# A decoder layer on one core: keys spread over four places, queries kept twice, x copied to PSUM by ScalarE, the maxima split in PSUM

## What is computed

```python
# 1. state-space mixer, 256 inner channels, 16 states each
x_h, res = split(layernorm(h) @ W_in.T);  x_h = silu(conv4(x_h))
dt, B, C = split(x_h @ W_x.T);            dt = softplus(dt @ W_dt.T + b_dt)
h_t = exp(dt_t * A) * h_{t-1} + dt_t * B_t * x_t          # scan over time
y_t = sum_states(h_t * C_t) + D * x_t
x = x + (inner residual) + alpha * (y * silu(res)) @ W_out.T
# 2. cross attention, 16 heads of 8 channels, 64 keys, masked
x = x + softmax(mask(q k^T / sqrt(8))) v @ w_o.T + b_o
# 3. eight experts, the two best of each token, 128 -> 512 -> 128 with relu
x = x + sum_top2(p_e * (relu(h W1_e + b1_e) W2_e + b2_e))
```

## Time and profile before

| | |
|---|---|
| median of 3 runs | 883.64 us (881.62 to 884.72) |
| the profiled execution | 876.18 us, its span 874.4 us |
| TensorE, matmuls | 693.3 us busy, 79% |
| VectorE | 714.5 us, 82% |
| ScalarE | 523.7 us, 60% |
| GpSimd | 629.3 us, 72% |
| mixer rounds | about 30 to 627 us |
| experts' groups, with the last attention | about 637 to 874 us |

### The profile page before, as it was taken

The page is one execution under the profiler, slowest core; times in us unless marked ns, Lnnn a source line. Parts: engine busy times, 40 slices in busy tenths (PEclk is TensorE's granted clock), DMA queues, the critical chain, the costliest instruction groups (busy, mean ns, idle before and its releaser), DMA issues. The chain is left out here.

```text
span 874.4 us, 12132 instructions
## 1 busy us (share of the span) xinstructions
PE 693.3 (79%) x3795; PEld 468.9 (54%) x3795; DVE 714.5 (82%) x1059; ACT 523.7 (60%) x1251; POOL 629.3 (72%) x467
## 2 busy tenths in 40 slices
PE   6567569778888787988878796776779889789991
PEld 4343335445555355545545553553457568689991
DVE  3679999999999999999999999999943644645684
ACT  3777549667966975887796697666125234223330
POOL 1358889688889898988988999898812334464554
PEclk9778869999999999999999999987899999899996
DMA  4535595463537447434632653654073325648773
GB/s 101 194 111 156 171 290 152 156 185 133 186 108 229 154 156 214 157 112 150 193 133 107 211 160 104 198 172 147 26 224 107 122 95 158 215 166 307 220 245 101
DMA packets 80410, 142.69 MB, mean 163 GB/s; under 512 B 10555, under 2 KB 53574, under 8 KB 80346
## 3 DMA queue, kind: packets, MB, share of 16 engines
q1 hardware_dynamic: 75802, 133.38, 48.1%
q0 software_dynamic: 4544, 8.54, 2.8%
HBM read 110.25 MB, written 37.27 MB: 169 GB/s over the span
## 5 line engine op out<-in xcount | busy, mean ns | idle before, releaser
L1451 POOL TENSOR_TENSOR prod<-hst,BC 128x1024 f32<-128x1024 f32 x128 | 301.5, 2362 | 65.0 <-DVE hst L1664 54.2
L1664 DVE TENSOR_TENSOR_SCAN hst<-dA,Rp 128x1024 f32<-128x1024 f32 x128 | 292.0, 2282 | 6.4
L1188 ACT ACTIVATE dA<-dtm,Aneg 128x255 f32<-128x255 f32 x512 | 214.2, 495 | 75.8 <-DVE hst L1664 74.9
L1571 POOL DMA_INDIRECT y2d<-prod,back x78 | 81.6, 1046 | 117.2 <-DVE prod L2016 101.3
L1456 POOL TENSOR_TENSOR prod<-prod 128x512 f32<-128x512 f32 x128 | 163.6, 1289 | 2.4
L1655 DVE TENSOR_TENSOR Rp<-BC,Rp 128x1024 f32<-128x1024 f32 x128 | 156.9, 1226 | 7.7 <-DMA BC<-bcd 0.6
L638 PE MATMUL Y<-prod,ident 128*128 128x256 f32 x512 | 139.1, 405 | 21.9 <-POOL prod L1456 17.0
L638 PEld LDWEIGHTS Y<-prod,ident 128*128 128x128 f32 x512 | 99.7, 202 | 57.1 <-POOL prod L1456 22.1
L638 PE MATMUL Mb<-hpad,winT 128*128 128x512 f32 (+1 forms) x176 | 83.2, 622 | 15.2 <-ACT xh L1137 11.9
L638 PEld LDWEIGHTS Rp<-BC,xh 128*128 128x128 f32 x624 | 76.0, 193 | 4.5 <-issue 2.6
L638 PE MATMUL Rp<-BC,xh 128*128 128x128 f32 x624 | 76.6, 276 | 0.6 <-DVE prod L2016 0.6
(11 more groups left out here) (266 smaller groups left out, 1170.4 us busy)
## 6 DMA issues: line engine op xcount, KB each, us to landing
BC<-bcd SPq DMA_DIRECT2D x63, 1024.0 KB, 5.6
BC<-recs SPq DMA_DIRECT2D x39, 578.0 KB, 4.2
xsd<-blank SPq DMA_DIRECT2D x17, 1056.0 KB, 12.0
dtm<-xsd SPq DMA_DIRECT2D x39, 132.0 KB, 3.8
recs<-in_L_ffn_W SPq DMA_DIRECT2D x16, 256.0 KB
xin<-in_x SPq DMA_DIRECT2D x8, 256.0 KB, 5.8
x2d<-x2o SPq DMA_DIRECT2D x8, 256.0 KB, 5.8
E<-x2d SPq DMA_DIRECT2D x4, 512.0 KB, 5.3
```

The costliest lines, as they stand in the source:

```text
L1188: m = A(dA[:, k % RING, i, 1:SEQ], dtm[:, r % 2, d, b * SEQ + 1:(b + 1) * SEQ], ACT.Exp, scale=Aneg[:, d, c * NC + i:c * NC + i + 1])
L1451: TT(prod[:, k % RING, :, :], hst[:, k % RING, :, :], BC[:, (k // 2) % BCR, 1, :, :], ALU.mult).then_inc(s_pd, 1)
L1571: pool.indirect_dma_start(out=y2d[:, :], out_offset=bass.IndirectOffsetOnAxis(ap=at, axis=0), in_=yr[:, j % YR, i, :], in_offset=None, bou ...
L1664: v.tensor_tensor_scan(hst[:, k % RING].rearrange("p n s -> p (n s)"), dA[:, k % RING].rearrange("p n s -> p (n s)"), U.rearrange("p n s - ...
```

## The change

- Kbd has 4 blocks in place of 16. Block j is KT times the sum of the four masks of heads j, 4 + j, 8 + j and 12 + j (`blk4`), so one block carries a head in each quarter of the channels. The queries are kept twice, qT[:, 0] and qT[:, 1], each with the channels of every second quarter zeroed (by `qscale` and `qbias`, per partition); the product of a 64-row half with copy w and the four blocks gives four heads. `scores` has four matmuls of 256 columns a tile instead of two of 512; `scores_t` takes the weights from the four blocks. The order of the heads in a bank changes (TRIO, `exps`).
- All `key_blocks` (four activations) stand at k = 6, in the drain at k = 7; `queries` issues two activations.
- `copy_xh` on ScalarE copies xh into DTX: for the second sequence in slot k = 6, ahead of `key_blocks`, once `inputs` of step 7 has read the old contents (s_u); for the next round's first one at k = 15, behind `decays`. `steps_x` waits for it (s_xc) and multiplies DTX by dtm in place.
- `steps_x`, `least` and `normed` move from VectorE's `middle` to its `slot`, behind the scan; `least` from k = 8 to k = 7.
- `split_max` writes the negated maxima as f32 into PSUM first (in the last round SBUF) and splits from there: five operations, where it was four.
- Five small constants are made at step 0 of round 0, and one (bq) goes.

```diff
-        TRIO = ((0, 1), (4, 5)), ((2, 3), (6, 7))
+        TRIO = ((0, 2), (4, 6)), ((1, 3), (5, 7))
...
-                    mm(T[h][:, :], qT[rows, b, t * P:(t + 1) * P], Kbd[rows, b, 8 * h:8 * h + 8, :], stop=False)
+                for w in range(2):
+                    for h in range(2):
...
+                        rows = slice(64 * h, 64 * h + 64)
+                        mm(T[h][:, w * SEQ:(w + 1) * SEQ], qT[rows, w, b, t * P:(t + 1) * P], Kbd[rows, b, :, :],
+                           start=w == 0, stop=False, skip_group_check=True)
...
-                A(qT[:, :, :].rearrange("p b s -> p (b s)"), T[1][:, :], ACT.Identity, bias=bq[:, 0:1], scale=float(HD) ** -0.5).then_inc(Ta.sem, 1)
+                for w in range(2):
+                    m = A(qT[:, w, :, :].rearrange("p b s -> p (b s)"), T[1][:, :], ACT.Identity, bias=qbias[:, w:w + 1], scale=qscale[:, w:w + 1])
+                m.then_inc(Ta.sem, 1)
...
+            def copy_xh(r, b):
+
+                if r or b:
+                    act.wait_ge(s_u, r * STEPS + b * (STEPS // 2))
+                    act.wait_ge(Aa.sem, Aa.at("xh1", r))
+                else:
+                    act.wait_ge(Ha.sem, Ha.at("xh1", 0))
+                A(DTX, xh[:, r % 2, :, b * SEQ:(b + 1) * SEQ], ACT.Copy).then_inc(s_xc, 1)
...
-                for h in range(half * HP, (half + 1) * HP):
-                    m = A(Kbd[:, :, h, :], KT[:, :, :], ACT.Copy, scale=blk[:, h:h + 1])
+                for j in range(HP // 2):
+                    m = A(Kbd[:, :, j, :], KT[:, :, :], ACT.Copy, scale=blk4[:, j:j + 1])
...
+                if k == 6 and r < ROUNDS:
+                    copy_xh(r, 1)
                 if prev and k == 6:
-                    key_blocks(r - 1, 0)
+                    key_blocks(r - 1)
...
+                if k == 15 and r + 1 < ROUNDS:
+                    copy_xh(r + 1, 0)
                 slot(r, k)
...
-                if r or b:
-                    v.wait_ge(s_u, r * STEPS + b * (STEPS // 2))
+                v.wait_ge(s_xc, r * NB + b + 1)
                 half = slice(b * SEQ, (b + 1) * SEQ)
-                v.tensor_tensor(DTX[:, :, :], dtm[:, r % 2, :, half], xh[:, r % 2, :, half], ALU.mult).then_inc(s_dx, 1)
+                v.tensor_tensor(DTX[:, :, :], dtm[:, r % 2, :, half], DTX[:, :, :], ALU.mult).then_inc(s_dx, 1)
...
-                v.tensor_scalar(nm[:, :, 0, 0:HEADS], mx[:, :, :], -1.0, None, ALU.mult).then_inc(Tv.sem, 1)
+                v.tensor_scalar(part, mx[:, :, :], -1.0, None, ALU.mult).then_inc(Tv.sem, 1)
                 v.wait_ge(Tv.sem, Tv.at("ma", r))
-                v.scalar_tensor_tensor(part, mx[:, :, :], -1.0, nm[:, :, 0, 0:HEADS], ALU.mult, ALU.subtract).then_inc(Tv.sem, 1)
+                v.tensor_copy(nm[:, :, 0, 0:HEADS], part).then_inc(Tv.sem, 1)
                 v.wait_ge(Tv.sem, Tv.at("mb", r))
+                v.tensor_tensor(part, part, nm[:, :, 0, 0:HEADS], ALU.subtract).then_inc(Tv.sem, 1)
...
+                if k == 7:
+                    steps_x(r, 1)
+                    if tail:
+                        least(r - 2)
+                if nxt and k == 15:
+                    steps_x(r + 1, 0)
+                if ln and k == 15:
+                    normed(r + 2)
```

More of the change, by code:

```diff
@@ L102, in decoder @@
         blk = sb("blk", [P, HEADS])
+        blk4 = sb("blk4", [P, HP // 2])
+        quads = sb("quads", [P, HP // 2])
         iota = sb("iota", [P, EXPERTS])
@@ L181, in decoder @@
         KT = sb("KT", [P, NB, KEYS])
-        Kbd = sb("Kbd", [P, NB, HEADS, KEYS])
+        Kbd = sb("Kbd", [P, NB, HP // 2, KEYS])
         Vg = sb("Vg", [P, NB, HP, GW])
         ones = sb("ones", [P, 2, GW])
-        qT = sb("qT", [P, NB, SEQ])
+        qT = sb("qT", [P, 2, NB, SEQ])
+        qscale = sb("qscale", [P, 2])
+        qbias = sb("qbias", [P, 2])
         sqt = sb("sqt", [P, TOK])
@@ L317, in decoder @@
         Ta = Marks(sem("Ta"), "KT V sq ln rs q m e00 e01 e10 e11 ld rd x2")
-        Tv = Marks(sem("Tv"), "xq " + " ".join(f"mx{i}a mx{i}b" for i in range(NB * QT)) + " ma mb mc me n")
+        Tv = Marks(sem("Tv"), "xq " + " ".join(f"mx{i}a mx{i}b" for i in range(NB * QT)) + " ma mb mc md me n")
         s_kb = sem("s_kb")
@@ L767, in scores @@
                 if i == 0:
-                    pe.wait_ge(s_kb, 2 * (r + 1))
-                for h in range(2):
[L770 to L774, removed]
-                    mm(T[h][:, :], qT[rows, b, t * P:(t + 1) * P], Kbd[rows, b, 8 * h:8 * h + 8, :], stop=False)
-                for h in range(2):
-                    mm(T[h][:, :], identb[:, :], mbias[:, t, :].unsqueeze(1).to_broadcast([P, 8, KEYS]), start=False).then_inc(Tp.sem, 1)
+                    pe.wait_ge(s_kb, r + 1)
+                for w in range(2):
+                    for h in range(2):
+                        if w == 0 and i:
+                            pe.wait_ge(Tv.sem, Tv.at(f"mx{i - 1}{'ab'[h]}", r))
+                        elif w == 0 and h == 0:
+                            pe.wait_ge(Ta.sem, Ta.at("q", r))
+                        rows = slice(64 * h, 64 * h + 64)
+                        mm(T[h][:, w * SEQ:(w + 1) * SEQ], qT[rows, w, b, t * P:(t + 1) * P], Kbd[rows, b, :, :],
+                           start=w == 0, stop=False, skip_group_check=True)
+                for h in range(2):
+                    mm(T[h][:, :], identb[:, :], mbias[:, t, :].unsqueeze(1).to_broadcast([P, 8, KEYS]), start=False, skip_group_check=True).then_inc(Tp.sem, 1)
             def turn_max(r):
@@ L789, in scores_t @@
                     for h in range(2):
-                        hp, rows = TRIO[g][h][i], slice(64 * h, 64 * h + 64)
-                        mm(T[h][:, i * SEQ:(i + 1) * SEQ], Kbd[rows, b, 2 * hp:2 * hp + 2, :], qT[rows, b, :],
+                        rows = slice(64 * h, 64 * h + 64)
+                        mm(T[h][:, i * SEQ:(i + 1) * SEQ], Kbd[rows, b, 2 * g:2 * g + 2, :], qT[rows, i, b, :],
                            start=i == 0, stop=False, skip_group_check=True)
@@ L1392, in _ @@
             first_half()
+            copy_xh(0, 0)
             act.wait_ge(s_pre, NPRE)
@@ L1773, in middle @@
                         logits(r - 2)
-                    if k == 8:
-                        least(r - 2)
                 if k == 11 and r < ROUNDS:
@@ L1781, in middle @@
                     maxima(r - 1, 2)
-                if k == 7 and r < ROUNDS:
-                    steps_x(r, 1)
-                if nxt and k == 15:
-                    steps_x(r + 1, 0)
-                if ln and k == 15:
-                    normed(r + 2)
             def slot(r, k):
@@ L1863, in _ @@
                 nxt_(v.tensor_copy(mbias2[:, t, :, :], mbias[:, t, :].unsqueeze(1).to_broadcast([P, 2, KEYS])))
-            nxt_(v.tensor_scalar(bq[:, :], bq[:, :], float(HD) ** -0.5, None, ALU.mult))
             assert n == NPRE
```

26 lines of the change are left out of this document (17 added, 9 removed).

## The result

The changed kernel takes **860.16 us** (median of 4 runs, 855.9 to 866.7), the kernel before 884.18 beside it (881.62 to 884.93): a ratio of 0.9746, 95% interval 0.9713 to 0.9778. Forecast were 859.6 us, 854 to 871. The profiled execution took 859.85 us, its span is 858.0.

A forecast was written before the change was run, and what follows sets the result against it. VectorE was taken to bound the round (72.77 of 75.10 us), GpSimd next. 17.5 + 1.6 + 5.9 - 1.8 + 0.8 = 24.0 us off the profile's 876.18 gives 852.2, plus 7.5 to the median: 859.6 us, range 854 to 871.

The forecast's parts named there:

- The stretch, 17.5 us: VectorE's dt*x: with x in PSUM, GpSimd can't hold it; 15 products fall from 27.7 to 10.2 us.
- The place, 1.6 us: `steps_x` behind the scan at k = 7 and 15: hides latency, 1.6 us gained beyond the stretch.
- the stretch isn't the operands: Rival at L1637 and L1688: they stretch because of where they stand, new ones alike; 883 us, chance 0.04.
- The split, 5.9 us: Maxima split on VectorE, rounds 1 to 7: five ops take 9.0 us where the old chain took 14.9.
- `least`, -1.8 us: VectorE at k = 7: `least` waits 0.3 us for GpSimd's `nl` in each of six rounds, losing 1.8 us.
- ScalarE's queue, slack 0 to 0.3 us: ScalarE at decays(10) behind `copy_xh`: fits narrowly; rival that it makes the kernel slower, 890 us, chance 0.06.
- The sign that I had named for going wrong: dA or the root named as a release before scans or `att_normed` at k = 9, 10.
- GpSimd's wait for the expert choice: GpSimd in the mixer round: its wait for VectorE's choice falls from 2.3 us to under 1.
- The drain, 0.8 us: Round 7's attention in the expert stage: fewer Kbd copies gain 1.0 us, the split's fifth op takes back 0.2.
- TensorE, 0: Scores as four 64x256 matmuls in place of two 64x512: same columns, costed at 0.
- The start, 0: Five constants at k = 0 of round 0, 1 us of work: taken as 0, at most 1.
- The sum: Whole kernel: the terms gain 24.0 us; 859.6 us forecast, chance 0.60.

The follow-up runs named there:

- e1: The changed kernel with the product dt*x reading x from SBUF again, copies, waits and place behind the scan kept: 860.87 us, ratio 0.9734.
- run 5: The changed kernel with dt*x back ahead of the scan, still in PSUM behind ScalarE's copy: 877.53 us, ratio 0.9997 to the kernel before.
- e12: The changed kernel with dt*x ahead of the scan, x from SBUF, no copies; new keys, queries and split stay: 876.44 us, ratio 0.9982.
- e3: The kernel before with only four Kbd copies, two query copies and matching score matmuls; old product and split: 879.72 us, ratio 0.9958.
- e6: The changed kernel with two more unread copies of 256 columns on ScalarE behind `copy_xh(r, 1)`: 862.96 us, ratio 0.982.
- e4: The kernel before with only `steps_x`, `least` and `normed` moved behind the scan, x from SBUF, no copy: 870.90 us, ratio 0.9841.
- e11: The changed kernel without `copy_xh` and its wait, dt*x behind the scan with x from SBUF: 852.02 us, ratio 0.9725.
- e10: The changed kernel with `key_blocks` two steps later and the first group table's small ops through PSUM: 853.61 us, ratio 0.9731.

## Why the prediction was right, point by point

**The stretch, 17.5 us.** The size was right: 28.4 to 10.8 us busy, 17.6. The cause was half right. Held ops with both operands in SBUF are shown (e1 at 350.56), and not holding them pays. That it takes the copy into PSUM to remove them is wrong: behind the scan the hold falls from 28.4 - 10.8 = 17.6 to 12.4 - 10.8 = 1.6 us without it. In the middle the operand does remove the hold (696 ns, run 5), but the waits for its copy eat all that it gives.

**The place, 1.6 us.** This step failed, by more than a factor of ten. I asked only what latency the old place exposed, and kept the stretch at the old operands' account; but the stretch itself depended on the place. Undone, it costs 21 us with the copies ((0.9997 - 0.9754) x 878) and 22.6 without them; done alone on the kernel before, it brings 12.5. My rival "the stretch isn't the operands" was drawn up wrongly for the same reason: it let the new ops stretch alike, as if they stood at the old place, so neither 883 us nor a product of 1.2 to 2.3 us could have shown that the place was at work. The forecast survived since both edits were made together, and their joint worth, 17.5 + 1.6, is about the 20 us ((0.9982 - 0.9754) x 878) that taking both away costs. As to how the gain divides between the two, that was luck.

**The split, 5.9 us.** Chain of 1.30 us seven times, 9.1, against 14.9: 5.8. Undone at the clock 6 to 7 us. Right, with a condition that I didn't see: while the product is still held, the split brings nothing (e12, which has it, 0.9982; e3, which hasn't, 0.9958), and in e12 VectorE waits 5.8 us for TensorE at its low clock.

**`least`, -1.8 us.** Wrong: 0.3 us in all. GpSimd's timeline after:

```profile
348.61 0.23 POOL L1490 TENSOR_TENSOR lg<-lg,x2o 128x32 f32<-128x32 f32 x1
348.92 0.25 POOL L1492 TENSOR_TENSOR nl<-bgn,lg 128x32 f32<-128x32 f32 x1
```

`nl` is over at 349.17, `least` starts at 349.89, 0.7 us later. I had moved GpSimd up by 1.70 only; counted from the split, it was over 360.87 + 0.25 - 318.09 = 43.03 us into the round and is now over 349.17 - 308.74 = 40.43, 2.6 us earlier. What I left out is that GpSimd's small ops had been held by the old product as well: `lg`, 0.23 us above, took 0.69 before.

```profile
360.11 0.69 POOL L1466 TENSOR_TENSOR lg<-lg,x2o 128x32 f32<-128x32 f32 x1
```

**ScalarE's queue, slack 0 to 0.3 us.** Right, and e6 measures it: about none. It went the right way only by the narrow margin. The sign that I had named for going wrong, the root before `att_normed` at k = 9, did come, in two of the six whole rounds (1.11 and 0.29 us, 1.4 in all), the long one by way of TensorE's clock, which the prediction has no term for. GpSimd's wait for the expert choice, which was to fall from 2.3 to under 1 us, is 0.8 and 0.9 in two of the rounds shown and 1.7 in that of 72.73. The copy of 512 columns into PSUM takes 0.59 us (mean of 16), 0.6 was taken.

**The drain, 0.8 us.** First expert op to the start of the last two maxima: 54.9 before, 54.1 in the changed kernel's profile, 51.6 in its second, 51.8 in e3. So it gave 0.8 us in one profile and 3.1 to 3.3 in two others: the term was right once and else too small by up to 2.5. I counted one wait of TensorE for the query and no later step behind the Kbd copies (VectorE's longest wait for the choice's exponentials, 2.6 us before, is 1.3 in e3 and 1.7 in the changed kernel's first profile); that this is the difference wasn't tested.

**TensorE, 0.** The matmuls cost no more at full clock, as taken (1.13 and 1.14 us). What I left out is the clock itself: the round with 0.60 over 3.20 us is about 1.5 us longer than the undisturbed ones (72.73 and 71.17). Over six rounds that is more than half of what parts the mean, 71.63, from the undisturbed 71.16.

**The start, 0.** The first whole round starts 2.5 us earlier than before (165.49 and 168.00), though the three products ahead of it alone take 3.5 us less; up to the 1 us that I allowed for may have been lost there.

**The sum.** In the profiles the last scan of the mixer's 128 ends at 603.85 us, before at 627.08: 23.2 us earlier, 20.8 of it in the six whole rounds, the rest ahead of them. (Before, these rounds took 74.59 to 75.50 us, 75.10 in the mean; they didn't "all have this period".) That the total came within 0.6 us of the forecast is luck: `least` gave 1.5 us more than forecast, the drain up to 2.5 more, and what is left of the mean round above the undisturbed one, 2.8 us in six rounds and half of it the clock's, took most of that back. The 7.5 us between profile and median, which I carried over, is not understood: the changed kernel's profile lies 0.3 below its median, so profile against profile the gain is only 16.3 us while medians move by 24.0. In the first expert tile and behind it the changed kernel's profile is 6.6 us longer (241.2 us to the end, before 234.6). VectorE's waits there, 730 to 770 us:

```profile
DVE xh L2039 <- remote: 7.4, 2, 4.0
DVE prod L2045 <- remote: 4.1, 2, 2.2
```

Nothing like them is in the profile of before, and the second profile of the changed kernel has 5.0 us of them and a tail of 236.6. Who released those waits the trace doesn't say, and no run was made for it: it stays open.

## What to carry to other kernels

An op that another engine's op holds up has two cures, other memory or another moment; before paying for the first, look in both timelines at which op starts first, and try moving the op to just behind the event that also releases the other engine. Ask of each part of a change what it is worth without the others: here two edits each removed the same stretch, and only the one without a copy to wait for could do it by itself. And a busy share of 80% says nothing of slack: 0.70 us of ScalarE at the wrong place cost about 0.8 a round.

## What the runs showed of the hardware that was not expected

- The same product, the same operands: 1757 to 1818 ns as a mean in the middle of the step (the kernel before, e3, e12), 760 to 917 behind the scan (e4, e11, e1).
- TensorE, idle for 4.24 us behind a stretch at full clock, was granted 0.50 of it over the next 6.84 us, and in the changed kernel an idle of 2.19 us was followed by 0.60 over 3.20, one of 2.25 in the round behind it by 1.00; eight matmuls of 256 columns took 2.67 us instead of 1.14. So releasing TensorE's work early, only to let it wait in the middle, can make it late at the end.
- An op on 128x8 values (`jump` from `goal`) took 2.27 us with its input in SBUF, from 607.51 to the end of GpSimd's product of 607.41, 2.35 us long, and 0.17 with its input in PSUM beside such a product (e10, at 598.28).
